# Second attention layer: fills between scores and transposes, and the first tile of each batch ranked by its 27 farthest keys in reversed order

## The reference

```python
att = einsum('bhqd,bhkd->bhqk', q, k) / sqrt(hd)          # 16 heads of 64, causal
S = maximum(att[:, 0], 0.0)                                # head 0; column 0 and diagonal set to 0
S_shifted = roll(S, 1, axis=-2).at[:, 0, :].set(0.0)
FF = cumsum(S_shifted, axis=-2)                            # grows with the query's row
att = att - FF[:, None]
memory_budget = max(1, int(T * 0.2))                       # 102 at 512 keys
sorted_idx = argsort(where(causal, FF, inf), axis=-1)
eff_k = minimum(memory_budget - 1, i + 1)                  # the 101 nearest keys, by FF
keep = <the first eff_k of sorted_idx> | eye               # all others are masked
y = softmax(where(keep, att, -inf)) @ v
y = y @ W_proj.T + b_proj
```

## Time and profile before

| what | value |
|---|---|
| median of 3 runs | 1010.16 us |
| the profiled execution's span | 1014.7 us |
| PE busy in it | 905.4 us (89%) |
| DVE busy | 734.6 us (72%) |
| ACT busy | 643.8 us (63%) |
| POOL busy | 537.6 us (53%) |
| MAX8 (L1355) in the second attention | 208, 103.1 us |
| MATCH_REPLACE8 (L1352) | 208, 99.9 us |
| first scores of the layer (L1227) | at 468.36 us |

### The profile page before, as it was taken

One profiled execution on the slowest core, in us unless ns is written; L12 is line 12 of the kernel. 1 busy time (PEld: TensorE's weight loads), 2 busy tenths in 40 slices (PEclk: granted clock), 3 DMA queues, 4 the chain that ended last, 5 costly groups with the idle time before them and its releaser, 6 DMA issues. The chain is left out here.

```text
span 1014.7 us, 19335 instructions
## 1 busy us (share of the span) xinstructions
PE 905.4 (89%) x6140; PEld 606.1 (60%) x6140; DVE 734.6 (72%) x2087; ACT 643.8 (63%) x1433; POOL 537.6 (53%) x664
## 2 busy tenths in 40 slices
PE   8899989998999999988999999989998988962396
PEld 5444444444678888865556666656665755652296
DVE  5676777763889999877997978697878878444022
ACT  2566656554778888844867677767777767740174
POOL 4234536243703344001668766877777778942344
PEclk9999999986999999999999999999999989985599
DMA  4000001000444433140000000000000000002882
GB/s 137 1 1 1 22 1 44 1 24 10 121 138 127 131 104 111 35 120 1 2 1 2 1 2 1 2 1 2 2 1 2 1 2 1 2 1 67 278 286 95
DMA packets 31130, 47.73 MB, mean 47 GB/s; under 512 B 3804, under 2 KB 18673, under 8 KB 30912
## 3 DMA queue, kind: packets, MB, share of 16 engines
q1 hardware_dynamic: 29104, 43.42, 14.2%
q0 software_dynamic: 1504, 3.17, 0.9%
q10 hardware_dynamic: 432, 0.01, 0.0%
HBM read 40.25 MB, written 6.79 MB: 46 GB/s over the span
## 5 line engine op out<-in xcount | busy, mean ns | idle before, releaser
L1507 POOL TENSOR_SCALAR probs<-probs,rinv 128x128 f32<-128x128 f32 (+3 forms) x256 | 274.7, 1086 | 102.1 <-DVE rinv L1372 102.0
L1442 ACT ACTIVATE probs<-probs,rowmin 128x128 f32<-128x128 f32 (+3 forms) x256 | 141.7, 559 | 30.1 <-DVE rowmin L1366 29.0
L1366 DVE CUSTOM_DVE_ANT_0 probs<-psum,adj 128x128 f32<-128x128 f32 (+3 forms) x256 | 122.2, 478 | 50.0 <-PE psum L1227 49.4
L1451 ACT ACTIVATE pt<-psum 128x128 f32<-128x128 f32 (+3 forms) x256 | 98.4, 435 | 69.1 <-PE psum L1237 66.9
L841 ACT ACTIVATE pT<-psum 128x1024 f32<-128x1024 f32 (+3 forms) x128 | 89.6, 702 | 61.9 <-PE psum L597 60.9
L1227 PE MATMUL psum<-k_sb,q_sb 64*128 64x256 f32 (+3 forms) x512 | 110.5, 484 | 17.5 <-DVE rowmin L1366 17.2
L769 DVE TENSOR_REDUCE top<-psum 128x2 f32<-128x256 f32 (+3 forms) x128 | 102.3, 818 | 19.7 <-PE psum L577 19.5
L1355 DVE MAX8 top<-w 128x8 f32<-128x131 f32 (+3 forms) x208 | 103.1, 496 | 4.6
L1815 ACT ACTIVATE r_hid<-psum,b1t 128x512 f32<-128x512 f32 x125 | 82.8, 689 | 33.0 <-PE psum L1654 28.8
L1237 PEld LDWEIGHTS psum<-ident,probs 128*128 128x128 f32 x640 | 68.4, 142 | 58.3 <-POOL probs L1507 37.6
L1237 PE MATMUL psum<-ident,probs 128*128 128x128 f32 x640 | 99.5, 286 | 0.8 <-POOL probs L1507 0.8
(11 more groups left out here) (306 smaller groups left out, 1914.1 us busy)
## 6 DMA issues: line engine op xcount, KB each, us to landing
r_share<-shares SPq DMA_DIRECT2D x12, 1024.0 KB, 7.1
s_wb<-in_w_all SPq DMA_DIRECT2D x23, 514.5 KB
sorted_x<-blank SPq DMA_DIRECT2D x1, 2967.0 KB, 11.9
s_xg<-sorted_x SPq DMA_DIRECT2D x23, 129.0 KB, 2.8
r_w1s<-in_w SPq DMA_DIRECT2D x16, 128.0 KB, 5.8
r_w2s<-in_w SPq DMA_DIRECT2D x16, 128.0 KB, 6.2
r_share<-shares SPq DMA_DIRECT2D x6, 256.0 KB, 3.4
r_share<-shares SPq DMA_DIRECT2D x2, 768.0 KB, 5.0
```

The source lines that it names most:

```text
L1366: dve.tensor_tensor_reduce(probs[:, k, 0:K], s_bank[h][:, 0:K], adj[:, OFF[i]:OFF[i] + K], 1.0, FLOOR, ALU.add, ALU.min, rowmin[:, k:k + 1 ...
L1442: act.activation(probs[:, k, 0:K], probs[:, k, 0:K], ACT.Exp, bias=rowmin[:, k:k + 1], scale=-1.0, accum_out=rsum[:, k:k + 1]).then_inc(ex ...
L1451: act.activation(pt[:, (2 * n + h) % 4, 0:K], t_bank[h][:, 0:K], ACT.Copy).then_inc(pt_ready, 1)
L1507: pool.tensor_scalar(probs[:, k, 0:K], probs[:, k, 0:K], rinv[:, k:k + 1], None, ALU.mult).then_inc(normed, 1)
```

## The change

It does three things. `pe_program` issues the fills of a step right after its scores, ahead of the transposes and products. `fills_at` puts an rs fill ahead of the step's other fills. And the first tile of each batch is ranked by its 27 farthest keys: w0 holds +FF (masked keys plus 1e37) written in reversed column order, 5 pad columns hold 1e38, 4 rounds mark 32 values, and GpSimd turns marked columns, read in reversed order, into the penalty. The planner deals the 8 instructions in place of 26.

```diff
-            PAD = -KEEP % 8
-            ROUNDS = (KEEP + PAD) // 8
+            SOUGHT = [P - KEEP if i == 0 else KEEP for i in range(NT)]
+            PAD = [-SOUGHT[i] % 8 for i in range(NT)]
+            RANKS = [2 * (SOUGHT[i] + PAD[i]) // 8 for i in range(NT)]
+            RANK_BASE = [t // NT * sum(RANKS) + sum(RANKS[0:t % NT]) for t in range(TILES + 1)]
...
                 if b + 1 < B:
+                    if l in RS_AT:
+                        out.insert(0, ("rs", b + 1, RS_AT.index(l)))
                     if l == X_AT:
                         out.append(("x", b + 1, 0))
...
-                    if l in RS_AT:
-                        out.append(("rs", b + 1, RS_AT.index(l)))
...
                         if n < NS:
                             pe_score(pe, n)
+                        for use in fills_at(n):
+                            pe_fill(pe, use)
                         if TURN_LAG <= n < NS + TURN_LAG:
                             pe_turn(pe, n - TURN_LAG)
                         if PV_LAG <= n < NS + PV_LAG:
                             pe_pv(pe, n - PV_LAG)
-                        for use in fills_at(n):
-                            pe_fill(pe, use)
...
-                        ins = dve.scalar_tensor_tensor(out=w0[:, WOFF[j]:WOFF[j] + K], in0=bank[:, 0:K], scalar=-1.0,
-                                                       in1=causal[:, N - K:N], op0=ALU.mult, op1=ALU.add)
+                        dst = w0[:, WOFF[j]:WOFF[j] + K]
+                        if j == 0:
+                            ins = dve.scalar_tensor_tensor(out=dst[:, ::-1], in0=bank[:, 0:K], scalar=1.0,
+                                                           in1=causal[:, N - K:N], op0=ALU.mult, op1=ALU.subtract)
+                        else:
+                            ins = dve.scalar_tensor_tensor(out=dst, in0=bank[:, 0:K], scalar=-1.0,
+                                                           in1=causal[:, N - K:N], op0=ALU.mult, op1=ALU.add)
...
-                k = (TILES - 1) * PER_TILE
+                k = len(RANK_STEPS)
                 for n in range(NS - 1, -1, -1):
                     RANKED_BY[n] = k
                     room = RANK_ROOM[n // PAIRS % NT] * (1.3 if n < SLOTS1 - PAIRS else 1.0)
-                    while k and n <= (1 + (k - 1) // PER_TILE) * PAIRS - 1 - RANK_EARLY and room > 0:
+                    while k and n <= RANK_STEPS[k - 1][0] * PAIRS - 1 - RANK_EARLY and room > 0:
                         k -= 1
-                        room -= RANK_COST[(1 + k // PER_TILE) % NT]
+                        room -= RANK_COST[RANK_STEPS[k][0] % NT]
...
-                                      ("rs", 0, 3): range(6, PER_TILE)}.get(use, ()):
+                                      ("rs", 0, 3): range(6, RANKS[0])}.get(use, ()):
...
-                    pool.tensor_scalar(w1[:, cols], w1[:, cols], TAKEN / 2, MASKED, ALU.is_gt,
+                    far, pen = w0[:, cols], w1[:, cols]
+                    if i == 0:
+                        far, pen = far[:, ::-1], pen[:, ::-1]
+                    pool.tensor_scalar(w1[:, cols], w1[:, cols], TAKEN / 2, MASKED, ALU.is_lt if i == 0 else ALU.is_gt,
                                        ALU.mult).then_inc(pen_step, 1)
```

More of the change, by code:

```diff
@@ L29 @@
 SENTINEL = 1e37
+FARTHEST = 1e38
 NOWHERE = 1 << 30
@@ L1022, in attention1 @@
             PV_LAG = 4
-            WOFF = [OFF[i] + PAD * i for i in range(NT)]
+            WOFF = [OFF[i] + sum(PAD[0:i]) for i in range(NT)]
             SCALE = -1.0 / math.sqrt(D1)
@@ L1112, in attention1 @@
                 rl = sbt("relu", [P, TOT])
-                w0 = sbt("w0", [P, TOT + PAD * NT])
-                w1 = sbt("w1", [P, TOT + PAD * NT])
+                w0 = sbt("w0", [P, TOT + sum(PAD)])
+                w1 = sbt("w1", [P, TOT + sum(PAD)])
                 top = sbt("top", [P, NT, 8])
@@ L1326, in dve_drain @@
                     ins.then_inc(f_dve, 1)
-                PER_TILE = 2 * ROUNDS
+                RANK_STEPS = [(t, k) for t in range(1, TILES) for k in range(RANKS[t % NT])]
                 RANKED_BY = [0] * NSTEP
-                k = (TILES - 1) * PER_TILE
+                k = len(RANK_STEPS)
                 for n in range(NS - 1, -1, -1):
@@ L1342, in dve_rank @@
                     r, take = divmod(k, 2)
-                    cols = slice(WOFF[i], WOFF[i] + P * (i + 1) + PAD)
+                    cols = slice(WOFF[i], WOFF[i] + P * (i + 1) + PAD[i])
                     src = w0 if r == 0 else w1
@@ L1349, in dve_rank @@
                     else:
-                        dve.wait_ge(ranked, t * PER_TILE + k)
+                        dve.wait_ge(ranked, RANK_BASE[t] + k)
                     if take:
@@ L1376, in dve_program @@
                         K = WOFF[i] + P * (i + 1)
-                        dve.memset(w0[:, K:K + PAD], SENTINEL).then_inc(preset, 1)
+                        dve.memset(w0[:, K:K + PAD[i]], FARTHEST if i == 0 else SENTINEL).then_inc(preset, 1)
                     dve.wait_ge(preset, NT)
@@ L1412, in dve_program @@
                             for k in range(done, RANKED_BY[n]):
-                                dve_rank(dve, 1 + k // PER_TILE, k % PER_TILE)
+                                dve_rank(dve, *RANK_STEPS[k])
                             done = RANKED_BY[n]
@@ L1488, in pool_penalty @@
                     cols = slice(WOFF[i], WOFF[i] + K)
-                    pool.wait_ge(ranked, (t + 1) * PER_TILE)
-                    pool.tensor_scalar(w1[:, cols], w1[:, cols], TAKEN / 2, MASKED, ALU.is_gt,
+                    pool.wait_ge(ranked, RANK_BASE[t + 1])
+                    far, pen = w0[:, cols], w1[:, cols]
+                    if i == 0:
+                        far, pen = far[:, ::-1], pen[:, ::-1]
+                    pool.tensor_scalar(w1[:, cols], w1[:, cols], TAKEN / 2, MASKED, ALU.is_lt if i == 0 else ALU.is_gt,
                                        ALU.mult).then_inc(pen_step, 1)
                     pool.wait_ge(pen_step, 2 * t + 1)
-                    blk = w1[:, WOFF[i] + P * i:WOFF[i] + K]
+                    blk = pen[:, P * i:K]
                     pool.tensor_tensor(blk, blk, notdiag[:], ALU.mult).then_inc(pen_step, 1)
@@ L1497, in pool_penalty @@
                         pool.wait_ge(biased, 2 * ((b - 1) * SLOTS1 + (i + 1) * PAIRS))
-                    pool.tensor_tensor(adj[:, OFF[i]:OFF[i] + K], w1[:, cols], w0[:, cols],
-                                       ALU.subtract).then_inc(adj_ready, 1)
+                    pool.tensor_tensor(adj[:, OFF[i]:OFF[i] + K], pen, far,
+                                       ALU.add if i == 0 else ALU.subtract).then_inc(adj_ready, 1)
                 def pool_norm(pool, n):
```

## The result

The changed kernel takes 1025.6 us (median of 4 runs, 1022.04 to 1031.95) against 1011.08 for the kernel before (4 runs, one more than in the 1010.16 above, 1009.35 to 1012.23): ratio 1.0145, 95% interval 1.0097 to 1.0194. It is slower, by 14.5 us where 22 were forecast.

What follows compares the result with a forecast made beforehand. It took VectorE to bind some steps, TensorE others. Ranking gave -7.0 us and fills waiting for ScalarE's drains +29.2, so 1010.2 + 22.2 = 1032 us; range 1013 to 1047, the forecast's own 1024 to 1041.

Steps and rivals of the forecast that it cites:

- part 2: Fills between scores and transposes: they wait for ScalarE's late drain of their bank, +29.2 us in sum.
- steps 8 to 24 of batch 0: Same fill waits as in later batches, 9.0 us, partly covered by VectorE's pace; half of 3.5 taken off: +7.2 us.
- start of the layer: Second v fill no longer waits behind VectorE's ranking, so the first scores come 1.4 us earlier.
- fourth tiles, ranking: Batches 0, 1, 2: ranking of steps 24 and 25 dropped, decay fill then late; 1.9 us gained per batch.
- steps 0 to 8 of batch 0: Two fills a step: steps 4, 5, 6 and the x fill of 7 wait 1.0 us each, +4.0.
- the same, batches 1 and 2: Steps 8 to 24: fills wait for ScalarE's drain of their bank, 9.0 us per batch, 18.0 together.
- Part 1: 4 ranking rounds in place of 13 for a batch's first tile: start and three fourth tiles, -7.0 us together.
- The fourth rival: VectorE is the bound throughout, all removed rounds count and no fill stalls: 989 us, chance 0.02.
- The price of one stall: TensorE's wait at a fill for ScalarE's drain: 1.0 us at 256 columns, 0.87 at 384, 1.0 at 128.
- Rival 1: ScalarE drains in time and no fill waits, so the kernel is faster: -7.0 us, 1003 us, chance 0.09.
- Rival 3: The chain spreads: second head's bias waits for exponentials, ranking slips behind it; +44 for the fills, 1047 us, chance 0.10.
- rival 2: Stalls are half the sum, since slack of one step covers the next: -7.0 + 14.6, 1018 us, chance 0.16.

Runs made afterwards that it cites:

- drain_own_step: Changed kernel, but ScalarE drains the fills of its own step first, not those of the step before: 1011.53 us, ratio to before 0.9979.
- ranks_only: Changed kernel with the fills back at the end of the step and rs last, so only the shorter ranking stays: 1004.93 us, ratio 0.9913.
- rs_first: Kernel before with the rs fill ahead of its step's other fills; one execution, only stretches used: steps 40 to 56 grow by 0.84 us.
- both_drains: drain_own_step plus VectorE draining rs and decay fills in their own step ahead of ranking, and planner room 1.9 for 2.6: 999.33 us, ratio 0.9892.
- ranks_spread: ranks_only with the planner's room in the fourth tile 1.9 in place of 2.6: 1002.19 us, ratio 0.9894.
- selective: ranks_spread with fills behind the scores only where no fill needs a bank of this step or the one before, not in step 8: 999.72 us.
- fills_only: Kernel before with the fills moved behind the scores and rs first, ranking as before: 1035.73 us, ratio 1.022.
- mixed: selective, with both_drains' order in steps 8 to 23 of batches 1 and 2: 998.45 us, ratio 0.9841.

## Why the forecast was right, and too high

The direction and the mechanism hold: part 2 puts TensorE behind a drain that stands late in ScalarE's order, and drain_own_step takes most of it away by moving the drain alone: 15.2 of the 19.5 us by which the changed kernel's layer is longer than that of ranks_only (first scores to step 126: 429.08, 413.86, 409.58). In steps 8 to 24 of batch 0 it takes away 0.9 of 5.5. The size by steps:

| term | forecast | changed kernel |
|---|---|---|
| start of the layer | -1.4 | -1.24 |
| fourth tiles, ranking (ranks_only) | -1.9 each | -1.9 each |
| fourth tiles, the moved fills | none | -0.6 each |
| steps 0 to 8 of batch 0 | +4.0 | +3.80 |
| steps 8 to 24 of batch 0 | +7.2 | +5.48 |
| the same, batches 1 and 2 | +9.0 each | +6.36, +6.41 |
| steps 32 to 40 and 64 to 72 | none | -0.33 each |
| steps 96 to 126 (the clock differs here too) | none | -0.52 |

Without rounding the right column is +12.0, where the forecast has +22.2.

- *Part 1* came out as worked: steps 24 and 25 at 2.7, step 26 still 5.04 us alone. The reversed operands, left open between nothing and double, cost nothing (last section). The decay fill is what is late, and VectorE's other rounds are worth little: 0.54 us a tile more when the ranking that is left is dealt evenly. The fourth rival is refuted for most steps: VectorE's removed rounds gave 1.9 us a batch of 6.6. It was drawn from the Trainium skill, "Perfetto Trace Analysis", section "Identifying the Most-Contended Engine", by whose weight-load share VectorE was the engine to relieve; the page names that share beside the share of peak arithmetic reached (MFU), which I left out. Where the row showed VectorE ahead of the scores it was the engine to relieve; a share over a stretch doesn't tell the two apart.
- *The price of one stall* was right where TensorE comes straight from the scores: 0.87 forecast, 0.96 of idle time in step 52, and step 52 longer by 0.89 (4.66 to 5.55). By groups in batch 1: steps 8 to 11 forecast 2.2, measured 2.13; steps 18 to 21 3.3 and 2.95.
- *The step that was off* is the sum over steps 12 to 16 of batch 1: 0.9 + 0.7 + 0.6 + 0.2 + 0.6 + 0.5 = 3.5 us forecast, and 17.60 to 19.18 us, 1.58, measured. TensorE had no idle time in these steps before. After, the k fill of step 12 waits 0.86 us (0.9 forecast), `out` of step 13 0.92 (1.3), the k fill of step 14 0.22 (0.6), and the q fills of steps 13 and 15 nothing (0.2 and 0.5): 2.00 us in all. I took off 0.4 to 0.5 for the rs fill that stands ahead in the same step; it covers more. TensorE in steps 13 and 14, and ScalarE's drain in step 14:

```profile
623.59 0.59 PE L1197 MATMUL psum<-k_sb,q_sb 64*128 64x256 f32 x2
...
625.11 2.05 PE L1218 MATMUL psum<-wo,yt 128*128 128x128 f32 x16 [0.92 <-ACT k_sb L1440]
...
628.81 0.70 PE L1230 MATMUL psum<-k_sb,q_sb 64*128 64x256 f32 x4
...
629.34 0.81 PE L1197 MATMUL psum<-k_sb,q_sb 64*128 64x384 f32 x2
...
629.64 0.68 ACT L1438 ACTIVATE q_sb<-psum,bqs 128x512 f32<-128x512 f32 x1
...
630.37 0.50 PE L1183 MATMUL psum<-xb_hi,wk_hi 128*128 128x512 f32 x1 [0.22 <-ACT q_sb L1438]
```

  The other 0.42 us is TensorE's work in these steps, which got shorter. The order of the rs fills shows no cost here, though it costs 0.82 us in the same steps of rs_first: in the changed kernel an rs fill stands right behind the scores, again beside work on 64 rows. both_drains, whose TensorE has the changed kernel's order, has no idle time in these five steps and takes 16.92 us, 0.69 less than before (its smaller room isn't the reason: ranks_spread takes 17.61). So the late drains cost 19.18 - 16.92 = 2.3 us here (both_drains moves those of both engines; the two aren't told apart).
- *The same for batch 1 as a whole:* of the 9.0 us forecast for steps 8 to 24, TensorE's idle time grew by 7.4 (0.36 to 7.79), and its work got 1.1 shorter: 6.36 measured.
- *Missed altogether:* a fill between scores and transposes costs TensorE 0.15 us less than one at the end of the step (below). It is the -0.6 of each fourth tile (four steps with a fill, 0.15 each), most of what steps 32 to 40 gain, and 0.4 in steps 9, 17 and 22.
- *Batch 0:* the cover by VectorE was taken as half of 3.5 us, 1.8; batch 0's stretch grew by 0.9 less than batch 1's.
- *Rival 1* is out: the fills do wait. Rival 3 too: the reciprocal waits for exponentials only 3.8 us in all, 1.6 before. The layer's +12.0 lies between the forecast's +22.2 and rival 2's +7.6, and nearer to the rival's. The stretches from step 0 to 24 alone grew by 22.05 of the 29.2; rival 2's reason, that something covers a stall, is shown where an rs fill stands between, and by the smaller growth of batch 0; the rest of the difference are the gains that were missed.
- *The time against the layer:* 14.5 us between the medians, 12.0 in the layer, 7.9 between the spans: in the profiled executions the stages ahead of the layer took 2.46 us less and those behind step 126 1.7 less. With the layer's 12.0 alone the time would have been 1022 to 1023 us, below the forecast's own range of 1024 to 1041; that 1025.6 lies in it is luck.

## What to carry to other kernels

Before work is moved ahead in one engine's order, look up where in the other engine's order the instruction stands that frees its buffer. Move both, or move only the work whose buffer is long free (selective). Moving both is no cure everywhere: steps 8 to 24 of batch 0 stayed 1.6 us above the kernel before. With two banks in turn and the drain one step late, a fill that goes ahead of the transposes waits for the exponentials, and holds up the transposes that feed them. Price such a wait per step with all that stands between, and measure by stretches from score to score: they were steady to 0.1 us at the same granted clock, where whole times scattered by several.

## What the runs showed of the hardware

**The joint behind a fill.** Weight loads and matmuls of TensorE, step 34 with the fill at the end (ranks_spread), then between scores and transposes (selective):

```profile
583.41 1.09 PE L1240 MATMUL psum<-ident,probs 128*128 128x128 f32 x8
584.44 1.09 PE L1256 MATMUL psum<-pt,v_sb 128*64 128x128 f32 x16
...
586.03 0.40 PE L1193 MATMUL psum<-wv_hi,xb_lo 128*128 128x512 f32 x1
586.36 0.49 PE L1230 MATMUL psum<-k_sb,q_sb 64*128 64x128 f32 x4
```

```profile
583.52 0.39 PE L1193 MATMUL psum<-wv_hi,xb_lo 128*128 128x512 f32 x1
583.75 1.03 PE L1240 MATMUL psum<-ident,probs 128*128 128x128 f32 x8
584.72 1.09 PE L1256 MATMUL psum<-pt,v_sb 128*64 128x128 f32 x16
```

From the fill's last matmul to the next work 0.33 us when the scores follow and 0.23 when transposes do, and from the transposes to the products 1.03 and 0.97: 0.16 in all. The step takes 3.37 and 3.20 us. The score's weight load stands with 0.36 us of idle that the profile calls issue, the transposes' has none. With the fill next to the transposes, both 128*128, the step has one change of matmul shape fewer; that this is what it saves was not tested.

**The granted clock in the last batch.** Windows of the kernel before (step 107 starts at 825.9), then of fills_only (its step 107 starts at 847.90); the clock is the number behind the five engines:

```profile
820.00:825.00 5.00, 3.31 (x25) 1.58 (x24) 4.86 (x21) 3.85 (x15) 3.03 (x5) 1.00 0.01 2
825.00:828.00 3.00, 2.12 (x12) 1.31 (x12) 2.96 (x14) 1.78 (x7) 1.83 (x2) 0.74 0.00 0
828.00:831.00 3.00, 2.92 (x16) 1.66 (x14) 2.95 (x12) 1.77 (x8) 2.50 (x3) 0.50 0.00 0
```

```profile
845.00:850.00 5.00, 3.10 (x22) 1.62 (x22) 4.90 (x20) 3.27 (x13) 3.65 (x4) 1.00 0.00 0
850.00:853.00 3.00, 2.37 (x20) 1.44 (x20) 2.97 (x12) 2.56 (x10) 2.60 (x3) 1.00 0.00 0
853.00:856.00 3.00, 3.00 (x30) 2.67 (x28) 2.93 (x11) 1.15 (x7) 2.83 (x4) 1.00 0.02 5
```

After steps in which TensorE was busy 3.31 of 5 us, waiting for VectorE, it was granted 1.2 GHz (0.50) in place of 2.4 for some 7 us. In fills_only it stayed at 2.4 behind a stretch in which TensorE was busy 3.10 of 5 us. Steps 108 and 109 take 3.25 + 4.53 us at the low level and 2.14 + 3.64 at the high one: 2.0 us. This falls differently from kernel to kernel, and is most of what moves the last batch between 84.0 and 87.1 us in the table; no difference there is put down to an edit.

**The granted clock ahead of the layer.** The stages ahead of the first rs fill are the same code in all ten kernels. They took from 446.97 us (both_drains) to 458.21 (mixed), at these granted clocks:

```profile
0.00:446.97 446.97, 411.94 (x2541) 266.57 (x2541) 346.64 (x577) 287.02 (x409) 175.30 (x278) 0.98 0.22 63
0.00:458.21 458.21, 426.65 (x2540) 273.19 (x2541) 347.42 (x577) 287.66 (x409) 175.25 (x278) 0.93 0.22 62
```

VectorE, ScalarE and GpSimd were busy alike, within 0.8 us; TensorE's busy time and the stretch went with the clock. The kernel before (453.13 us at 0.95) and the changed one (450.67 at 0.96) lie between. The four executions of the changed kernel go the same way: 1022.04 us at 0.951, 1024.43 at 0.949, 1026.77 at 0.943 and 1031.95 at 0.935. So the scatter of the whole times goes with the clock; why one execution is granted more than another is not shown.

**Reversed operands.** GpSimd's sum of penalty and decay for a batch's first tile, before, then with both operands read in reversed order in the changed kernel (the second number behind the first bar is the mean in ns):

```profile
L1498 POOL TENSOR_TENSOR adj<-w 128x128 f32<-128x128 f32 x4 | 1.8, 461 | 0.3
```

```profile
L1507 POOL TENSOR_TENSOR adj<-w 128x128 f32<-128x128 f32 x4 | 1.8, 457 | 0.3
```

VectorE's decay write in reversed order takes 279 to 291 ns, 284 on average in order before. At 128 columns of f32 the reversal cost nothing. (Two of GpSimd's three instructions for such a tile have reversed operands, not three as forecast.)
